# Removing a small scaling step, moving two steps of the first batch, and a wider bias row in a fused cross-attention kernel

## What is computed

```python
# block 0: attention over channels x positions
q = einsum('bcn,dc->bnd', x, Wq) + bq          # d = 64
k = einsum('bcn,dc->bdn', x2, Wk) + bk[:, None]
v = einsum('bcn,dc->bdn', x2, Wv) + bv[:, None]
attn = softmax(einsum('bnd,bdm->bnm', q, k), axis=2)
x = einsum('bcm,bnm->bcn', v, attn) + x
# block 1 (its x_2 is the same context): no softmax
g_x, theta_x, phi_x = conv1x1(g_w, x_2), conv1x1(theta_w, x), conv1x1(phi_w, x_2)
y = (theta_x^T phi_x / N) g_x                   # CI = 256
out = batchnorm(conv1x1(w_w, y)) + x
```

## Time and profile before

| what | value |
|---|---|
| median of 3 runs | 1047.39 us (1045.72 to 1047.51) |
| the profiled execution's own time | 1045.72 us |
| its span (first to last instruction) | 1043.8 us |
| PE busy | 1029.1 us (99%) |
| DVE / ACT / POOL busy | 678.7 / 495.2 / 293.4 us |
| HBM traffic | 84 GB/s over the span |

### The profile page before, as it was taken

One profiled execution on the slowest core, in us unless ns is written; L12 is line 12 of the kernel. 1 busy time (PEld: TensorE's weight loads), 2 busy tenths in 40 slices (PEclk: granted clock), 3 DMA queues, 4 the chain that ended last, 5 costly groups with the idle time before them and its releaser, 6 DMA issues.

```text
span 1043.8 us, 13884 instructions
## 1 busy us (share of the span) xinstructions
PE 1029.1 (99%) x5055; PEld 852.4 (82%) x5055; DVE 678.7 (65%) x970; ACT 495.2 (47%) x835; POOL 293.4 (28%) x253
## 2 busy tenths in 40 slices
PE   8979999999999999999999999999999999999998
PEld 6768887888878888888878888788887888878887
DVE  6976287843788448883488825888267872688625
ACT  7643365434644355442655427444175441655421
POOL 1651262112611127012260123602244021530220
PEclk9989999999999999999999999999999999999999
DMA  7525352261613615245142452424423343333502
GB/s 254 156 56 139 118 200 56 71 184 72 206 40 85 219 35 188 48 106 190 59 164 60 115 169 71 152 67 120 157 91 132 79 123 143 120 102 81 131 31 81
DMA packets 80916, 121.94 MB, mean 117 GB/s; under 512 B 13136, under 2 KB 46800, under 8 KB 80848
## 3 DMA queue, kind: packets, MB, share of 16 engines
q1 hardware_dynamic: 71632, 104.26, 32.6%
q10 hardware_dynamic: 9216, 16.78, 5.1%
HBM read 70.66 MB, written 16.78 MB: 84 GB/s over the span
## 4 chain that ended last, share of the span: by engine, by line
PE 86%; DVE 7%; ACT 3%; POOL 2%; issue 1%; DMA 0%; SPq 0%; ACTq 0%; DVEq 0%; POOLq 0%
PE pG L654 33%; PE pG L560 11%; PE pG L665 8%; PE pG L568 5%; PE pG L599 5%; PE pT L687 4%; PE pG L687 4%; PE pG L575 4%; DVE acc L906 3%; PE pS L611 2%; PE pM L633 2%; PE pM L642 2%; DVE pT L926 2%; PE pT L611 2%; ACT x2Ts L785 1%
## 5 line engine op out<-in xcount | busy, mean ns | idle before, releaser
L654 PE MATMUL pG<-pt,vT 128*128 128x512 f32 x1536 | 353.8, 389 | 0.0
L654 PEld LDWEIGHTS pG<-pt,vT 128*128 128x128 f32 x1536 | 286.8, 188 | 58.6
L1095 POOL TENSOR_TENSOR xms<-xr,xms 128x512 fp32r<-128x512 f32 x64 | 87.4, 1370 | 328.3 <-ACT xms L847 328.3
L560 PE MATMUL pG<-wv,x2s 128*128 128x512 f32 x720 | 169.1, 392 | 1.1 <-DVE vT L939 0.5
L560 PEld LDWEIGHTS pG<-wv,x2s 128*128 128x128 f32 x720 | 133.9, 188 | 32.5 <-issue 2.5
L1011 DVE SCALAR_TENSOR_TENSOR xr<-pG,cl,xr 128x512 f32<-128x512 f32 x64 | 47.6, 749 | 172.4 <-PE pG L654 172.4
L847 ACT ACTIVATE xms<-xr 128x512 fp32r<-128x512 f32 x64 | 40.4, 631 | 175.1 <-DVE xr L1011 174.8
L988 DVE TENSOR_TENSOR pt<-mv,pt 128x512 fp32r<-128x512 f32 x128 | 82.8, 689 | 52.2 <-ACT pt L825 51.8
L1091 POOL TENSOR_TENSOR ys<-yf,ys 128x256 fp32r<-128x256 f32 x32 | 29.2, 913 | 283.1 <-ACT ys L816 283.1
L825 ACT ACTIVATE pt<-mv 128x512 fp32r<-128x512 f32 x128 | 73.4, 623 | 59.1 <-DMA mv<-tp 38.1
L1066 POOL TENSOR_TENSOR x2Ts<-x2T_f,x2Ts 128x512 fp32r<-128x512 f32 x64 | 83.7, 1335 | 49.0 <-ACT x2Ts L785 49.0
(11 more groups left out here) (145 smaller groups left out, 1479.3 us busy)
## 6 DMA issues: line engine op xcount, KB each, us to landing
mv<-tp SPq DMA_DIRECT2D x512, 64.0 KB, 2.0
x2T_f<-in_ctx2T_dram SPq DMA_DIRECT2D x32, 512.0 KB, 4.6
xr<-in_x_dram ACTq DMA_DIRECT2D x64, 256.0 KB, 4.4
st<-in_ctx_dram SPq DMA_DIRECT2D x31, 512.0 KB, 6.3
st<-in_x_dram SPq DMA_DIRECT2D x29, 512.0 KB, 4.1
out_dram<-oh SPq DMA_DIRECT2D x32, 256.0 KB, 2.0
out_dram<-xr SPq DMA_DIRECT2D x31, 256.0 KB, 7.9
x_raw<-in_x_dram SPq DMA_DIRECT2D x3, 512.0 KB, 7.9
```

Source lines behind the costliest of these rows:

```text
L560: last = mm(bank, x2s[:, l, c, 128 * m:128 * m + 128], wv[:, r, c, :], start=(c == 0 and n == 0), stop=(c == 3 and n == 2))
L654: last = mm(bank, vT[:, l, m, 128 * c:128 * c + 128], pt(h)[:, r, m, :], start=(m == 0 and n == 0), stop=(m == 7 and n == 2))
L1095: done(tt(xms(h)[:, c, LO, :], xr[c][:, :], xms(h)[:, c, HI, :].bitcast(F), ALU.subtract), "xlo")
```

## The change

- The step `s8`, its tile `scol8` and its eight places in POOL's order (one in `FIRST`, one in `LATER` for each other batch) go. `br` becomes 512 wide: the loaded row stays in the first half and POOL writes the scaled row to the second. `acc` reads the second half and Y the first, with `scol` for `scol8`.
- In the first batch `psi` moves on PE from behind S:7 to ahead of Y:0.
- In the first batch `w:8` moves on ACT from behind S:7 to between Y:0 and Y:1.
- The filler of 640 bytes and the assertion go; with the wider `br` all regions from `ra` on begin 352 bytes later.

```diff
 FIRST = dict( pe=(
-        "GT:1 v:7 S:5 Y:0 Y:1 Y:2 S:6 S:7 psi Y:3 PV:0,0,0 ..."
+        "GT:1 v:7 S:5 psi Y:0 Y:1 Y:2 S:6 S:7 Y:3 PV:0,0,0 ..."
 act=(
-        "S:3 T:0 G:1 G:2 T:1 G:3 GT:0 S:4 GT:1 acc w:7 v:6 v:7 T:2 S:5 T:3 Y:0 Y:1 Y:2 S:6 Y:3 psi S:7 w:8 xr:0 "
+        "S:3 T:0 G:1 G:2 T:1 G:3 GT:0 S:4 GT:1 acc w:7 v:6 v:7 T:2 S:5 T:3 Y:0 w:8 Y:1 Y:2 S:6 Y:3 psi S:7 xr:0 "
 pool=(
-        "x2T:0 ... x2T:7 acc s8 Y:0 Y:1 ..."
+        "x2T:0 ... x2T:7 acc Y:0 Y:1 ..."
 LATER = dict( pool=(
-        "x1:0,0 ... x1:3,1 s8 x2T:0 ..."
+        "x1:0,0 ... x1:3,1 x2T:0 ..."
-        br = at("br", [128, 256], F, o); o += 1024
+        br = at("br", [128, 512], F, o); o += 2048
-        scol8 = at("scol8", [128, 4], F, o); o += 32
-        o += 640
-        assert (o - base) % 512 == 0
-            eng.dma_start(br[:, :], brow[0:256].partition_broadcast(128)).then_inc(s_bd, 16)
+            eng.dma_start(br[:, 0:256], brow[0:256].partition_broadcast(128)).then_inc(s_bd, 16)
 # DVE, do_acc
-                             in1=acc(b)[:, :] if n else br[:, :], op0=ALU.mult, op1=ALU.add), "acc")
+                             in1=acc(b)[:, :] if n else br[:, 256:512], op0=ALU.mult, op1=ALU.add), "acc")
 # DVE, do_Y
-                if c == 0:
-                    wait(eng, "s8", b)
-                done(stt(out=yf[:, c, :], in0=br[:, :], scalar=scol8[:, c:c + 1], in1=bank_of(G_Y + c)[:, 0:256],
+                if b == 0 and c == 0:
+                    eng.wait_ge(s_bd, 16)
+                done(stt(out=yf[:, c, :], in0=br[:, 0:256], scalar=scol[:, c:c + 1], in1=bank_of(G_Y + c)[:, 0:256],
 # POOL
-            def do_s8(b):
-                wait(eng, "x2sum", b, 3)
-                done(eng.tensor_scalar(scol8[:, :], scol[:, :], 128.0 / N, None, ALU.mult), "s8")
-                eng.tensor_scalar(br[:, :], br[:, :], N / 128.0, None, ALU.mult).then_inc(s_br8, 1)
+                eng.tensor_scalar(br[:, 256:512], br[:, 0:256], N / 128.0, None, ALU.mult).then_inc(s_br8, 1)
```

## The result

The changed kernel takes 1053.37 us in the median (1052.23 to 1053.7), against 1047.45 us: a ratio of 1.0058, 95% interval [1.0041, 1.0076], 6 us slower. The forecast was 1047.1 us with a range to 1052.2.

The account below looks back on a forecast made before the run. PE's matmul pace was taken to bound the kernel from the second batch on. Terms 0 + 0 - 0.33 (psi) + 0 + 0 = -0.33 us gave 1047.1 us against the 1047.39 median; range 1044.9 to 1052.2 us.

Parts of the forecast that it names:

- Parts 1 and 2: On POOL, dropping the small s8 operation and giving the scaled bias row its own place: covered by waits, 0 us each.
- Part 3: First batch on PE: psi's two matmuls fit in the 6.79 us hole ahead of Y:0, gaining 0.33 us.
- Part 4: First batch on ACT: w:8 earlier removes a 2.28 us DVE stall that PE was not waiting for, 0 us.
- Part 5: All tiles from ra on move 352 bytes: taken as 0 us, bounded by 40 us for PE and 2.2 us for transfers.
- Rival (b): Shifted starts slow PE's reads from the second stage on: 1 ns per matmul, 5.1 us, giving 1052.2 us; chance 0.15.
- The far bound: Upper limit for the layout on PE: widest difference between same-shape rows, 7.9 ns over 5055 matmuls, 40 us.
- (c): Transfers slow at the start, where first matmuls hang on loads: up to +2.2 us, 1049.3 us; chance in full 0.10.
- the sign chosen for (b): In PE's timeline, 24 matmuls of line 654 taking more than 5.47 us would show slowed reads.
- The sign that did catch it: A batch taking 0.3 us more or less than before would by itself undo the forecast, as there are seven.

## Why the prediction was wrong

What bounds the kernel was read rightly: only the pace of the matmuls could move the end from the second batch on, and that is where the 6 us came from.

Parts 1 and 2 (s8, the bias row): 0 forecast. After the change POOL still waits for ACT before its first x2T half of the third batch, 1.74 us against 1.67; its timeline:

```profile
277.38 1.50 POOL L1063 TENSOR_TENSOR x2Ts<-x2T_f,x2Ts 128x512 fp32r<-128x512 f32 x1 [1.74 <-ACT x2Ts L782]
```

With the moved steps these parts stand in the 1.3 us of the change without the shift; alone they were not run.

Part 3 (psi): -0.33 us forecast. Psi fits in the hole, starts at 64.51 and holds nothing up, as forecast. The whole of parts 1 to 4 came out at -1.3 us, with 0.3 to 2.2 as the interval, and psi with w:8 at -0.6 (-1.6 to +0.3), so the sign is right and the size is of the order of what can be measured.

Part 4 (w:8): 0 forecast; the copy runs at 71.15, the second ys copy goes from 72.00 to 72.10, DVE's stall is gone and PE sees nothing. The step stands.

Part 5 (the layout) is the step that failed, and the failure is in one sentence: "where a tile lies seems not to matter, so I take 0". It rested on wo in the unmoved part and PV's operands in the moved part having one pace. But that row compared tiles that all lay alike, a multiple of 256 bytes from one another, so it could say nothing of a distance that isn't such a multiple. The question was put to single tiles, whether a start at an odd multiple of 32 bytes costs anything, and the experiment with everything shifted shows that it doesn't. What moved was the distance between the two operands of one matmul: 6 to 7.5 ns more on v, k, q, theta and B (96 + 16 + 16 + 48 + 12 = 188 of a batch's matmuls), +8 us alone. The prediction also called the moved tiles nearly everything that PE streams; but v, Y and B stream weights, which stayed, and so meet moved tiles as their stationary operand.

Rival (b) had the right place ("the shifted starts slow PE's reads") and a chance of 0.15, but its price, 1 ns on each matmul, was picked to give a number and not from a row. That its +5.1 us came near the measured +6 is luck: what slowed was three matmuls in ten, by about 6.7 ns each, and the others kept their pace. The far bound of 7.9 ns per matmul was near the size of the single price, but over all 5055 matmuls it gives 40 us. With 7.4 us (1.06 us, seven times) in place of 0 the sum would have been 7.4 - 0.33 = +7.1 us, inside the measured interval (+4.3 to +8.0).

Two more slips stand beside it. The upper end of the range was said to hold (b) at 1 ns and all of (c), but those add up to 1047.1 + 5.1 + 2.2 = 1054.4 us, not 1052.2, which is (b) alone; the measured 1053.37 us lies between the two. And the sign chosen for (b), 24 matmuls of line 654 in more than 5.47 us, would have missed it: PV has both operands in the moved part, and its 24 took 5.46 us. The sign that did catch it was the batch, 1.06 us longer where 0.3 was the limit.

The Trainium skill ("SBUF — State Buffer", Specifications and the note on cachelines) counts SBUF lines of 16 bytes. Shifts of 32, 96 and 128 bytes are whole multiples of that and cost 5.8 to 6.7 ns per matmul of theta here, so for this effect the measurement differs from what I drew from the page. The rule on transfers that start off a 256-byte boundary ("DMA: Bandwidth & Descriptors", How a descriptor splits into AXI transactions) would have been visible at most in the moves, whose landing stayed at a median of 2.0 us. Their last pair is converted by 227.57 + 1.29 = 228.86 us in the second batch, 3 us ahead of PE, so no such cost reached the end. Rival (c), slower loads at the start, didn't come either: PE's idle time before 35 us is 35.00 - 31.66 = 3.34 us in the change's profile and 35.00 - 31.29 = 3.71 us in that before. The row of the last pair:

```profile
227.57 1.29 DVE L985 TENSOR_TENSOR pt<-mv,pt 128x512 fp32r<-128x512 f32 x2 [2.45 <-ACT pt L822]
```

What stays open is what in the chip has this period. That the streamed operand and the next stationary one are read at once and get in each other's way is a guess; no run separates the two reads.

## What to carry to other kernels

Bytes that come or go in a hand-made memory map are a change of their own: list which pairs of tiles meet in one instruction, and work out by how much their distance changes, before any other term. A row that shows "no effect" bears only on what varied in it. Where an engine sets the pace over the whole span, a few ns per instruction outweigh every stall of a first stage. A term for such a pace that no row shows is an open question and not a 0, and the ends of a range should be added up like the forecast.

## What the runs showed of the hardware

- float32r matmuls of 512 columns, stationary and streamed operand a multiple of 256 bytes apart in SBUF: 226.7 ns each (theta, B). At 32, 96, 128 or 224 bytes: 232.5 to 234 ns. At 64 bytes 229.0 ns if the streamed tile lies later (theta), 233 if the stationary one does (B).
- Shifting both by the same 352 bytes: 226.7 ns.
- Matmuls of 256 columns (Y): 125.0 ns at 0, 125.3 at 96, 119.4 at 64 bytes with the stationary tile later, and 118.9 with one weight alone placed so; here a distance can help.
- The low clock around the first batch's hole of 5 to 7 us ended between 69.5 and 72.1 us in ten traces with one PE order, and between 69.8 and 72.3 us in four with the other.
